# Attention of a fused layer: score chunks outermost, denominators by products with ones, three banks for maxima

## The reference, cut to what matters

```
qkv = bn(conv1x1(gn(x)))                     # 3*256 channels
qkv -> (B*AREA=16 areas, 1024 positions, 8 heads, 96)
q, k, v = qkv[..., :32], qkv[..., 32:64], qkv[..., 64:]
attn = softmax(einsum('bhdn,bhdm->bhnm', q, k) * 32**-0.5)
out  = einsum('bhdm,bhnm->bhdn', v, attn)
x = x + proj(out + pe(v));  x = x + deform_conv(gn(x), ...)
```

## Time and profile before

| | |
|---|---|
| median of three runs | 5404.09 us |
| profiled execution | 5400.96 us, its span 5399.1 us |
| attention loop, first to last maximum rows | 177.7 to 2705.5 us |
| last half and its end | to 2795 us |
| granted clock of TensorE, mean | 0.914 |
| busy share PE, DVE, ACT, POOL over the span | 79%, 72%, 44%, 60% |

### The profile page before, as it was taken

The page is one execution under the profiler, slowest core; times in us unless marked ns, Lnnn a source line. Parts: engine busy times, 40 slices in busy tenths (PEclk is TensorE's granted clock), DMA queues, the critical chain, the costliest instruction groups (busy, mean ns, idle before and its releaser), DMA issues. The chain is left out here.

```text
span 5399.1 us, 77451 instructions
## 1 busy us (share of the span) xinstructions
PE 4287.8 (79%) x18884; PEld 1801.9 (33%) x18884; DVE 3862.5 (72%) x6758; ACT 2389.6 (44%) x4441; POOL 3256.1 (60%) x1968
## 2 busy tenths in 40 slices
PE   1888888888888888888848989596878778787888
PEld 0222222222222222222216665233444344443444
DVE  5888888887887878878820018127888888888888
ACT  1355555555555555555430005333444444444444
POOL 0476676666766666766641112116777777777776
PEclk9799999999999998999968999798999999999999
DMA  4111111111111111111138877778999999999998
GB/s 157 38 51 38 49 43 45 57 47 42 47 39 51 56 37 44 48 45 52 36 104 202 188 181 288 225 200 324 380 366 367 370 358 380 368 374 362 383 370 342
DMA packets 338610, 966.19 MB, mean 179 GB/s; under 512 B 53536, under 2 KB 119712, under 8 KB 323792
## 3 DMA queue, kind: packets, MB, share of 16 engines
q0 software_dynamic: 165888, 604.05, 29.0%
q1 hardware_dynamic: 172368, 358.24, 22.9%
HBM read 805.78 MB, written 104.96 MB: 169 GB/s over the span
## 5 line engine op out<-in xcount | busy, mean ns | idle before, releaser
L403 POOL TENSOR_TENSOR psum<-psum,pr 128x1024 f32<-128x1024 f32 x576 | 1492.8, 2610 | 416.3 <-ACT pr L471 407.4
L515 DVE TENSOR_REDUCE nmx<-mring 128x1 f32<-128x512 f32 x2048 | 1303.6, 680 | 445.5 <-PE mring L647 437.9
L1370 POOL DMA_INDIRECT gat<-gather_table,idc x1152 | 1346.7, 1169 | 431.3 <-issue 346.2
L471 ACT ACTIVATE pr<-ering 128x512 f32<-128x512 f32 x2048 | 1149.5, 598 | 1005.1 <-PE ering L667 1000.4
L1486 PE MATMUL pac<-smt,wds 128*128 128x512 f32 x2304 | 1092.6, 619 | 25.1 <-ACT smt L1385 24.8
L647 PE MATMUL mring<-ks,qs 96*128 96x512 f16 x2048 | 866.2, 423 | 248.5 <-DVE nmx L515 241.1
L667 PE MATMUL ering<-qs,ks 98*128 98x512 f16 x2048 | 830.7, 414 | 162.3 <-DMA qs<-mlo 123.2
L1438 DVE SCALAR_TENSOR_TENSOR pbb<-gat,wtc,pa 128x256 f32<-128x256 f32 x1152 | 514.3, 479 | 270.4 <-ACT pa L1395 241.3
L1385 ACT COPY smt<-ptr 128x512 f32<-128x512 f32 x576 | 335.9, 583 | 787.5 <-PE ptr L1498 786.7
L1498 PE MATMUL ptr<-cst,sm 128*128 128x128 f32 x2304 | 374.2, 288 | 338.2 <-DVE sm L1452 337.7
L679 PE MATMUL acc<-pr,vt 128*32 128x512 f32 x4096 | 604.1, 665 | 0.0
(11 more groups left out here) (133 smaller groups left out, 3094.1 us busy)
## 6 DMA issues: line engine op xcount, KB each, us to landing
toep<-toe SPq DMA_DIRECT2D x64, 896.0 KB, 10.6
gather_table<-pix SPq DMA_DIRECT2D x64, 512.0 KB, 8.4
va<-v_pixel_major SPq DMA_DIRECT2D x40, 512.0 KB, 11.8
gat<-gather_table,idc POOLq DMA_INDIRECT x1152, 6.4
xs<-xa SPq DMA_DIRECT2D x16, 1024.0 KB, 4.7
xin<-xa SPq DMA_DIRECT2D x16, 1024.0 KB, 4.8
qs<-qkh SPq DMA_DIRECT2D x256, 64.0 KB, 2.0
ks<-qkh SPq DMA_DIRECT2D x256, 64.0 KB, 2.0
```

Source lines behind the costliest of these rows:

```text
L403: gp.tensor_tensor(psum[:, g, h, :], pr[:, 0, h, :] if m == 1 else psum[:, g, h, :], pr[:, m % 2, h, :], ALU.add).then_inc(s_pa, 1)
L471: act.activation(pr[:, m % 2, h, c * 512:(c + 1) * 512], ering[n % 2][:, :], ACT.Exp).then_inc(s_e, 1)
L515: dve.tensor_reduce(nmx[:, g, n // CH, n % CH:n % CH + 1], mring[n % 2][:, :], AX.X, ALU.max, negate=True).then_inc(s_mf, 1)
L1370: gp.indirect_dma_start(gat[:, r, :, :].rearrange("p q c -> p (q c)"), None, tab, bass.IndirectOffsetOnAxis(ap=idc[:, e, u:u + 1], axis=0) ...
```

## The change

- The 512-wide chunk c of the queries becomes outermost in a half: 16 slots for chunk 0 over all eight key tiles, then 16 for chunk 1. A slot still makes two score products, now of two heads of one chunk. `pr` has eight buffers by key tile, each of 4 x 512.
- `psum` is the sum of two neighbouring key tiles (`add_pair`, 4 x 512 wide), made by POOL alone, eight in a half, in two buffers. PE multiplies each by ones and accumulates in the new bank `den`, four for each chunk (`denominators`, every fourth slot).
- `acc` takes one bank. The bank won and one of `wring` become a third bank of maxima and `den`; `wbank` is the only one for qk tiles, v tiles and the transpose.
- The denominators are inverted chunk by chunk (`invert`), the result is divided by POOL (`divide`) and stored by chunk (`store_out`).
- The low parts of q and k are subtracted by POOL (`split`), after its additions 4 and 5 of a half.
- DVE splits the maxima from PSUM in two operations instead of three.
- SP's queue: the inversion of chunk 0 stands ahead of the stacking of the next area, and of the rows of maxima.

The diff, cut to its core:

```
-            mring = [pb(st, f"mring{n}", [P, 512]) for n in range(2)]
-            wring = [pb(st, f"wring{n}", [P, 512]) for n in range(2)]
-            acc = pb(st, "acc", [P, CH, 512])
+            mring = [pb(st, f"mring{n}", [P, 512]) for n in range(3)]
+            wbank = pb(st, "wbank", [P, 512])
+            acc = pb(st, "acc", [P, 512])
+            den = pb(st, "den", [P, 512])
...
+            QK_AT = (NT + 3, NT + 11)
+            STEPS = NT * CH
+            SUMS = STEPS // 2
+            CSUMS = SUMS // CH
+            DEN_AT = 8
+            NUM_SLOT = (SLOTS // CH + 1, 1)
+            DEN_SLOT = (DEN_AT + 4 * (CSUMS - 1) + 1, DEN_AT + 4 * (SUMS - 1) + 1 - SLOTS)
+            R_SLOT = (DEN_SLOT[0] + 4, DEN_SLOT[1] + 5)
+            Y_SUM = (7, 3)
+            QL_SUM = (4, 5)
...
                     def body(i, odd, first, last):            # SP
                         if not last:
                             sp.wait_ge(s_xn, i + 1)
                             load_x(i + 1)
+                        if not first:
+                            invert(i - 1, 1, 1)
                         sp.wait_ge(s_ve, i * NT + NT)
                         for g in range(HG):
                             store(v_d[g], i, vt[:, g, :, :], s_vout)
                         if not first:
-                            fold_den(i - 1, 1)
-                            spread_recip(i - 1, 1)
-                            sp.wait_ge(s_yo, i * (HG * CH))
-                            store(ya_d, i - 1, yo_all, s_out)
+                            store_out(i - 1, 1, 1)
+                        invert(i, 0, 0)
                         if not last:
                             stack(i + 1, 1 - odd, 0)
                         max_rows(i, odd, 1)
-                        fold_den(i, 0)
-                        spread_recip(i, 0)
+                        store_out(i, 0, 0)
+                        invert(i, 0, 1)
+                        store_out(i, 0, 1)
+                        invert(i, 1, 0)
                         if not last:
                             stack(i + 1, 1 - odd, 1)
                             max_rows(i + 1, 1 - odd, 0)
+                        store_out(i, 1, 0)
...
+                    def add_pair(i, g, k):                    # POOL
+                        gp.wait_ge(s_e, i * (HG * EXN) + (E0 + g * EXN + (k + 1) * 2 * HQ))
+                        if k >= 2 or g or not isinstance(i, int) or i:
+                            gp.wait_ge(s_den, i * (HG * SUMS) + (g * SUMS + k - 1))
+                        m = 2 * k % NT
+                        gp.tensor_tensor(psum[:, k % 2], pr[:, m], pr[:, m + 1], ALU.add).then_inc(s_pa, 1)
...
+                            for k in range(SUMS):
+                                add_pair(i, g, k)
+                                if k == 1 and g == 0 and not last:
+                                    gp.wait_ge(s_v, i * NT + NT)
+                                    normalise(i + 1)
+                                if k == Y_SUM[1] and not (first and g == 0):
+                                    divide(*before)
+                                if k == Y_SUM[0]:
+                                    divide(i, g, 0)
+                                if not last and k in QL_SUM:
+                                    split(i + 1, g, QL_SUM.index(k))
...
-                        dve.tensor_scalar(mrow[:, g, :], wring[1 - g][0:HQ * NT, 0:P], 1.0 / MS, None,
-                                          ALU.mult).then_inc(s_tt, 1)
-                        dve.tensor_copy(mhi[:, g, :], mrow[:, g, :]).then_inc(s_ms, 1)
-                        dve.tensor_tensor(mlo[:, g, :], mrow[:, g, :], mhi[:, g, :], ALU.subtract).then_inc(s_ms, 1)
+                        dve.tensor_scalar(mhi[:, g, :], wbank[0:HQ * NT, 0:P], 1.0 / MS, None,
+                                          ALU.mult).then_inc(s_ms, 1)
+                        dve.scalar_tensor_tensor(mlo[:, g, :], wbank[0:HQ * NT, 0:P], 1.0 / MS, mhi[:, g, :],
+                                                 ALU.mult, ALU.subtract).then_inc(s_ms, 1)
...
-                        if t >= 2:                            # PE, v_tile
-                            pe.wait_ge(s_ve, i * NT + (t - 1))
+                        if t:
+                            pe.wait_ge(s_ve, i * NT + t)
...
-                        m, h, c = n // (HQ * CH), n // CH % HQ, n % CH
+                        c, m, h = n // (NT * HQ), n // HQ % NT, n % HQ
...
+                                if slot % 4 == 0:             # PE, between the two pairs of a slot
+                                    k = (slot - DEN_AT) // 4
+                                    if k >= 0:
+                                        denominators(i, g, k)
+                                    elif not (first and g == 0):
+                                        denominators(*before, k + SUMS)
```

More of the change, by code:

```diff
@@ L372, in _ @@
                     over_areas(sp, body)
[L373 to L377, removed]
+                    invert(NA - 1, 1, 1)
+                    store_out(NA - 1, 1, 1)
+                    for c in range(CH):
+                        sp.wait_ge(s_out[c], 16 * NA * HG)
                     sp.wait_ge(s_vout, 16 * HG * NA)
@@ new lines, in body @@
+                            before = (i, 0, 1) if g else (i - 1, 1, 1)
+                            for slot in range(SLOTS):
+                                step = slot // 2
+                                if slot % 2 == 0 and not (first and g == 0 and step < NT):
+                                    weights_free(i, g, step)
+                                for x in range(2):
+                                    n = slot * 2 + x
+                                    act.wait_ge(s_s, i * (HG * EXN) + (g * EXN + n + 1))
+                                    act.activation(pr[:, step % NT, n % HQ, :], ering[n % 2][:, :],
+                                                   ACT.Exp).then_inc(s_e, 1)
+                                if slot == NUM_SLOT[0]:
+                                    copy_num(i, g, 0)
+                                if slot == DEN_SLOT[0]:
+                                    copy_den(i, g, 0)
+                                if not (first and g == 0):
+                                    if slot == NUM_SLOT[1]:
+                                        copy_num(*before)
+                                    if slot == DEN_SLOT[1]:
+                                        copy_den(*before)
+                                if not last:
+                                    for n in share(slot, *QK_AT, QKN):
+                                        qk_evac(i + 1, g, n)
@@ new lines, in denominators @@
+                    def denominators(i, g, k):
+                        pe.wait_ge(s_pa, i * (HG * SUMS) + (g * SUMS + k + 1))
+                        if k % CSUMS == 0 and (g or k or not isinstance(i, int) or i):
+                            pe.wait_ge(s_dn, i * (HG * CH) + (g * CH + k // CSUMS))
+                        for h in range(HQ):
+                            mm = pe.matmul(den[HD * h:HD * h + HD, :], ones[:, :], psum[:, k % 2, h, :],
+                                           start=k % CSUMS == 0, stop=k % CSUMS == CSUMS - 1,
+                                           tile_position=(0, HD * h))
@@ L718, in body @@
                                         v_tile(i, t)
-                                if not (first and g == 0):
-                                    if slot == DSLOT:
-                                        denominators(*before, g and last)
+                                if slot % 4 == 0:
[4 more added lines that the diff above has]
+                                        denominators(*before, k + SUMS)
+                                pair(1)
                                 if not last:
```

308 lines of the change are left out of this document (122 added, 186 removed).

## The result

The changed kernel takes 5476.88 us, the median of 4 runs (5463.10 to 5480.16), against 5397.81 us of the kernel before on the same chip (4 runs): ratio 1.015, 95% interval [1.0111, 1.0188]. It is 1.5% slower. The forecast was 5515 us with a range of 5370 to 5680 and 79% for slower. The profiled execution took 5475.76 us, its span is 5474.0 us.

What follows compares the result with a forecast made beforehand. No engine was full, so waits between engines bound the kernel. Areas +132, last area −12, end −6 and prologue −2 gave +112 on 5401.0 us, the median 3 us above: 5515 us, range 5370 to 5680.

Steps and rivals of the forecast that it cites:

- The chain behind T24: End of a half: SP free at T24 + 7.8, stacking 16.1, then 2.6 us; next half starts at T24 + 26.5.
- Both gates: Before stacking: split 1 on POOL, done at T24 + 7.4, and SP's inversion of chunk 0, through at T24 + 7.8 us.
- T24: Start of slot 24 of a half's 32: forecast 54.3 us in group 1, 63.7 in group 0, mean 59.0.
- segments of group 1: Its half cut at slot starts: 26.3 us to T12, 18.7 to T19, 9.3 to T24.
- wrong if T24 is below 55 us: One of the signs named beforehand that would show the forecast wrong.
- The area: Two halves of the attention loop: 171.9 us against 163.1, +8.8, times 15 areas +132.
- The third rival: POOL's additions take longer, 5.9 to 7.1 us instead of 4.7: 5600 to 5705 us; chance 24%.
- this term: Group 0, single wbank: PE waits 0.9 us for vt before four of eight v tiles, 3.6 us.
- The last area and the end: Last area stacks nothing, group 0 69.6 us instead of 81.5: −12; PE's final wait for POOL's additions: −6.
- The prologue: Ahead of the loop: first 64 maxima with three banks, less the slower splits: −2 us, within 5.
- The sum: Whole kernel: +112 us on the profiled 5401.0 us, giving a median of 5515 us.
- The second rival: Stacking hides, SP through before T32: a half 72.2 us, an area 145.3, total 5115 us; chance 6%.

Runs made afterwards that it cites:

- The two single edits: Each on the changed kernel: splits behind additions 3 and 4 (5493.85 us), or only the fold ahead of stacking, reciprocals behind the maximum rows (5441.85 us).
- the one with both: Changed kernel with splits behind additions 3 and 4, only the denominators' fold ahead of stacking, and reciprocals behind the maximum rows: 5257.96 us, ratio 0.9736.
- the run with a second v bank: Changed kernel with two maximum banks instead of three, the freed bank given to the v tiles, which alternate between two: 5511.62 us, ratio 1.0208.
- the fastest kernel: The one with both, now with both splits after addition 3 and the fold between stacking of head 0 and heads 1 to 3: 5117.52 us, ratio 0.9462.

## Why the prediction was right, step by step

- **The chain behind T24.** Forecast T24 + 26.5; measured 26.7 and 25.85, in the mean 27.0 and 25.9. Both gates lay as read: SP free at T24 + 8.1 (forecast 7.8), split 1 at T24 + 6.5 (forecast 7.4). The two single edits and the one with both showed that these are two parallel gates. What the forecast had wrong here costs nothing: PE's own last eight slots were put at 11.7 us (their terms add up to 11.2) and its wait at nearly 15; it is busy for 13.26 and waits 11.4 to 13.7, since the stacking ends when it ends.
- **T24.** Forecast 54.3 and 63.7; measured 53.3 and 64.4. By segments of group 1 it is 24.4, 19.4 and 9.5 against 26.3, 18.7 and 9.3, of group 0 35.5 to T12 against 35.7. The 1.9 us by which the first segment of group 1 came sooner are the third maximum bank: the sum put nothing down for it there, and with two banks that segment takes 25.9 to 26.2 us, as forecast. From T12 to T24 it was the other way round: 29.0 us in both groups instead of 28.0, although the third bank gives 1.2 us there. So part of the agreement of the mean, 58.9 against 59.0, is luck: an advantage that was not counted and a stretch that was put too short cancel. The sentence "wrong if T24 is below 55 us" was meant for the mean, which is 58.9; group 1 alone was always forecast below.
- **The area.** Forecast 171.9, measured 170.3 ((2739.94 − 185.47) / 15), so +108 instead of +132 over 15 areas. Of the 1.6 us, 0.9 is the pause at the loop's branch, which the sum added to every area beside both chains; 0.3 is T24, 0.4 the chain.
- **POOL.** Forecast 4.7 with 7.1 as the other end; measured 4.52 in the mean over 256 additions. The third rival is out. The Trainium skill (GPSIMD Engine Reference, section 1, Specifications) names DVE instructions with two SBUF inputs or in a two-port mode as those that contend. This trace agrees: beside DVE's reductions from PSUM all 256 additions took 4.49 to 4.55 us.
- **DVE.** Forecast about 42 us a half, measured 43.5. PE waited for vt 65 times in 16 areas, 4.1 of the eight tiles in each, and the run with a second v bank gives this term 3.4 to 3.6 us, as forecast.
- **The last area and the end.** The last half of group 0 was forecast at 69.6 us, measured 69.4. Behind its mlo, the end was forecast 6 us shorter and is 13.3 shorter (89.6 to 76.3): only the 7.9 us of PE's last wait (10.58 to 2.70) were thought of, and cut to 6. The rest is that a single chunk is left at the end: its last products take 1.06 us instead of 3.64, and the way from its copy to the end of the stage 13.5 instead of 16.2.
- **The prologue.** Forecast −2 within 5, measured +7.7 (177.74 to 185.47). This term was wrong in sign and outside its bounds. The first stacking begins 9.6 us later (104.48 to 114.06). The step that failed is that only the slower splits were counted against the change there. They are 0.9 us of it (2.12 us for the last one instead of 1.22). The other 8.5 are the single `wbank`: ahead of the loop the qk tiles follow each other with nothing in between, and each now waits for ACT's copy of the one before. PE's timeline in the changed kernel:

```profile
92.33 3.75 PE L623 MATMUL wbank<-xn,wqk 128*128 128x512 f32 x4 [25.15 <-DVEq L545]
97.62 3.78 PE L623 MATMUL wbank<-xn,wqk 128*128 128x512 f32 x4 [1.54 <-ACT qkh L474]
```

  ACT's last copy of these four tiles starts at 110.96 us instead of 102.43. No run took the term apart; this is read from the two traces.
- **The sum.** Attention ends 90.5 us later (108.4 − 12.3 − 13.3 + 7.7) instead of 112. The later stages were 15.5 us shorter in this profile, which lies within the spread of the profiles and was in no term. The mechanism held; the sizes of the area and of the end were 31 us too high and the prologue's 10 us too low.
- **The second rival** was not this kernel. Its price, 5115 us if stacking hides, lies beside the 5117.5 of the kernel that puts the splits and the inversion out of the way, but the terms differ: there T24 is at 57.3 us in the mean instead of 59.0 (58.8 in the changed kernel), and the half lasts another 15.8 instead of 13.2, since stacking does not hide wholly. That the two numbers meet is luck in part.

## What to carry to other kernels

When a transfer stands in a hand-written queue behind another chain's wait, both chains' lengths add up there: read the queue's order before the engines' busy shares, and ask which of the two the next stage needs first. If two gates end within a microsecond or two of each other, removing one shows little (0 and 1.0 us a half here, 7.5 for both); change both before judging either. A pause of PE can cost more than its length, since the stretch behind it may run at a lower clock. Here that part did not shrink with the pause from 11.9 to 4.3 us, and mostly went at 1.6.

## What the runs showed of the hardware

- A DVE instruction on 128 elements a partition took 1.97 to 2.35 us with SBUF sources alone beside POOL's additions (31 each of mhi and mlo in the kernel before) and 0.27 to 0.28 us with a PSUM source, in the changed kernel and, with nothing else altered, in the one before, where POOL's additions went on as ever. In the trace of the kernel before the two engines line up:

```profile
1559.72 2.36 POOL L403 TENSOR_TENSOR psum<-psum,pr 128x1024 f32<-128x1024 f32 x1
1559.87 2.35 DVE L532 TENSOR_TENSOR mlo<-mrow,mhi 32x128 f16<-32x128 f32 x1
```

  In all 31 halves mlo begins 0.15 us after an addition of POOL and ends 0.15 us after it, and mhi ends 0.08 us behind the addition ahead of that one. The one pair that DVE made while POOL stood idle, ahead of the loop, took 0.21 and 0.28 us from the same sources. So DVE stands still until POOL is done.
- POOL's addition of 128x2048 was within 4.49 to 4.55 us for all 256, once DVE ran no additions; at 128x1024 beside them it ranged from 2.33 to 3.54.
- Behind a pause PE starts at the lower clock level (1.2 GHz). Over the 12 slots behind it the changed kernel was granted 0.87 to 0.95 of full speed (two profiles), after pauses of 11.4 to 13.7 us; the kernel with both edits 0.82 to 0.95, after 3.2 to 6.0 us; the fastest kernel 1.00 in 19 of 30 halves and 0.88 to 0.95 in the others, after 0.6 to 3.1 us. Equal work took 32.6 us at 1.00 and 35.5 at 0.91.
- 24 stacking transfers take SP 15.1 to 17.2 us in the changed kernel, 15.2 in the median, which is 0.63 us for each. At 72.9 us a half this is a fifth of SP's time and the longest piece of the chain behind T24.
